# Attention and routed feed-forward on one core: rewritten for 32-row head groups, with the second half of the products for the maxima in front of the output projection

## The reference

```python
# x, ctx: (128, 128, 256), 128 batch elements of 128 tokens; 16 heads of 16 columns
q = (layernorm(x) @ Wq.T + bq) * 16 ** -0.5
k, v = ctx @ Wk.T + bk, ctx @ Wv.T + bv            # heads split
x = x + (softmax(q @ k.T) @ v) @ Wo.T + bo
# routed FFN on the 16,384 tokens, 32 experts, hidden 64
n = layernorm(x)
e = argmax(n @ router_w.T + router_b)
x = x + relu(relu(n @ w1[e] + b1[e]) @ w2[e] + b2[e])
```

## Time and profile before

| | |
|---|---|
| median of 3 runs | 2137.03 us (2135.17 to 2138.63) |
| span of the profiled execution | 2137.2 us, 51280 instructions |
| PE busy | 1898.6 us (89%) x18624 |
| PEld busy | 1418.2 us (66%) x18624 |
| DVE busy | 1553.0 us (73%) x4242 |
| ACT busy | 1209.9 us (57%) x2241 |
| POOL busy | 604.0 us (28%) x532 |
| granted clock of PE in 40 slices | tenths: 8, 7, then 9 up to slice 31, 6, and 5 in the last eight |

### The profile page before, as it was taken

The page is one execution under the profiler, slowest core; times in us unless marked ns, Lnnn a source line. Parts: engine busy times, 40 slices in busy tenths (PEclk is TensorE's granted clock), DMA queues, the critical chain, the costliest instruction groups (busy, mean ns, idle before and its releaser), DMA issues.

```text
span 2137.2 us, 51280 instructions
## 1 busy us (share of the span) xinstructions
PE 1898.6 (89%) x18624; PEld 1418.2 (66%) x18624; DVE 1553.0 (73%) x4242; ACT 1209.9 (57%) x2241; POOL 604.0 (28%) x532
## 2 busy tenths in 40 slices
PE   3699998989898989898989989898999399999998
PEld 2577776767676767676767767676777266666665
DVE  4488888878888888788878888888887444444443
ACT  2476666667666667666766666666667022222222
POOL 4112222222232222222222222222310134444444
PEclk8799999999999999999999999999999655555555
DMA  7800000111111110001000000011000333333320
GB/s 267 280 21 32 32 31 32 36 35 33 32 41 32 41 32 31 32 31 32 31 32 32 32 32 31 32 39 35 31 11 12 85 100 100 100 100 99 98 72 22
DMA packets 64060, 119.28 MB, mean 56 GB/s; under 512 B 8433, under 2 KB 45692, under 8 KB 63614
## 3 DMA queue, kind: packets, MB, share of 16 engines
q1 hardware_dynamic: 44734, 60.65, 9.5%
q0 software_dynamic: 19072, 55.15, 7.4%
HBM read 60.65 MB, written 59.31 MB: 56 GB/s over the span
## 4 chain that ended last, share of the span: by engine, by line
PE 63%; DVE 21%; issue 11%; POOL 3%; DMA 1%; DVEq 0%; SPq 0%; POOLq 0%; another core or an unknown queue 0%; ACT 0%
PE sc L812 13%; PE sc L988 9%; PE b L980 8%; PE b L826 6%; DVE mx L492 5%; DVE work L558 5%; PE sc L810 5%; PE b L773 4%; PE b L833 4%; PE b L973 3%; PE sc L791 3%; PE b L847 3%; PE b L782 2%; DVE rz L534 2%; DVE st L549 1%
## 5 line engine op out<-in xcount | busy, mean ns | idle before, releaser
L385 ACT ACTIVATE qM<-qT,cst 128x512 fp32r<-128x512 f32 x1024 | 640.0, 710 | 0.0
L812 PE MATMUL sc<-qM,kT 128*128 128x512 f32 x1536 | 518.8, 432 | 0.0
L310 POOL DMA_INDIRECT pages<-row,slot_i x128 | 129.0, 1008 | 1183.5 <-DVE slot_i L635 1151.1
L395 ACT ACTIVATE pv<-sc 128x512 f32<-128x512 f32 x512 | 295.6, 594 | 127.1 <-PE sc L812 122.0
L492 DVE TENSOR_REDUCE mx<-sc 128x4 bf16<-128x512 f32 x512 | 318.0, 684 | 53.1 <-issue 39.3
L812 PEld LDWEIGHTS sc<-qM,kT 128*128 128x128 f32 x1536 | 254.5, 193 | 16.5
L343 POOL DMA_INDIRECT out<-work x160 | 193.2, 1207 | 237.0 <-DVE work L725 234.2
L810 PEld LDWEIGHTS sc<-mxT,sel_b 128*128 128x128 bf16 x2048 | 116.7, 98 | 172.9 <-issue 124.1
L810 PE MATMUL sc<-mxT,sel_b 128*128 128x128 bf16 x2048 | 204.9, 223 | 25.1 <-DVE mxT L529 25.0
L534 DVE RECIPROCAL rz<-b 128x256 f32<-128x256 f32 x128 | 223.7, 1748 | 0.7 <-PE b L826 0.7
L988 PE MATMUL sc<-xs,rz 65*128 65x256 f32 x320 | 195.2, 714 | 0.0
(11 more groups left out here) (119 smaller groups left out, 3158.7 us busy)
## 6 DMA issues: line engine op xcount, KB each, us to landing
pages<-empty POOLq DMA_DIRECT2D x8, 2600.0 KB, 23.2
work<-pages SPq DMA_DIRECT2D x40, 520.0 KB, 3.9
xs<-x_in SPq DMA_DIRECT2D x32, 512.0 KB, 3.5
work<-ctxT SPq DMA_DIRECT2D x32, 512.0 KB, 3.3
out<-work POOLq DMA_INDIRECT x160
pv<-w SPq DMA_DIRECT2D x1, 2080.0 KB
w1s<-w SPq DMA_DIRECT2D x1, 2064.0 KB
pages<-row,slot_i POOLq DMA_INDIRECT x128
```

What stands on the lines that cost most here:

```text
L385: ins = act.activation(qM[:, u % 2, :, :, h, :], qT[:, par, :, :, u * P:(u + 1) * P].bitcast(F32), ACT.Copy, scale=cst[:, C_MASK + h:C_MAS ...
L395: act.activation(pt[:, u % 2, j], sc[j][:, :], ACT.Exp).then_inc(S["exp_out"], 1)
L812: ins = pe.matmul(sc[j][:, :], kT[:, par, a, c, u * P:(u + 1) * P], qM[:, u % 2, b, c, 4 * (j % 2):4 * (j % 2) + 4, :].rearrange("p h t -> ...
```

## The change

**Attention.** Heads are taken by row groups of 32 rows (`32 * g`), two heads to a group with two masks: `qM` is no longer eight masked copies but two, made straight from the projection with a scale and a bias, and `kT` and `qM` are plain fp32 without low parts. `scores` is eight fp32 matmuls (16 instructions) of 32 rows, 128 columns, 256 wide; `subtract_max` sixteen bf16 ones of 32 rows; `scores_for_max` two halves of eight bf16 ones of 32 rows into two banks (`mb`), the first half early in the unit, **the second directly in front of `project_out`**. `attend` is sixteen matmuls; the ones stand in `vs` beside the values, so that sums come out in the same product, and DVE normalises (`normalise`): a 32x32 block transpose of 128x512, a reciprocal of 128x16, a product, a transpose back of 128x256. The copy of the values and both norms' rows move to ACT, the router's places mostly to POOL, the residual comes two units late. The stage's loop has four steps to a turn instead of two, and the empty pages are written in pieces by SP (40 ahead, then 4 a step) and no longer all by POOL at the start.

**Pages.** The second weights stay in SBUF and TensorE reads the expert's number into a register; the first weights of a page come from HBM by a DMA of SP (`load_w1`, a ring of eight), which reads the number too. Both are padded, so that every matmul of a page has 128 rows and 128 columns. DVE copies no weights any more.

```diff
+            def load_w1(n, r, first):
+                if not first:
+                    apart(sp, ("h_out", n - (W1R - 1)))
+                e = sp.value_load(table[0:1, bass.ds(n, 1)], min_val=0, max_val=E - 1)
+                sp.dma_start(w1p[:, r % W1R, 0:2 * HID + 1],
+                             w1[:, bass.ds(e, 1), :].rearrange("p e h -> p (e h)")).then_inc(S[f"w1_in{r % W1R}"], 16)
+
...
-            def masks(q, par, u, at):
...
-                for h in range(8):
-                    ins = act.activation(qM[:, u % 2, :, :, h, :], qT[:, par, :, :, u * P:(u + 1) * P].bitcast(F32), ACT.Copy,
-                                         scale=cst[:, C_MASK + h:C_MASK + h + 1])
-                ins.then_inc(S["mask_out"], 1)
...
+                    for m in range(2):
+                        ins = act.activation(qM[:, par, m, c], pA[:, :], ACT.Identity,
+                                             scale=cst[:, C_MASK + m:C_MASK + m + 1], bias=bqm[:, m, c:c + 1])
+                ins.then_inc(S["proj_out"], 1)
...
+            def normalise(q, u):
                 after(dve, "PV_done", 4, q, u)
-                dve.reciprocal(rz[:, :], b7[:, 2 * P:4 * P]).then_inc(S["inv_out"], 1)
+                dve.transpose(tr[:, :], pB[:, :]).then_inc(S["tr_out"], 1)
+                after(dve, "tr_out", 4, q, u)
+                dve.reciprocal(inv[:, :], tr[:, :].rearrange("p (k r) -> p k r", r=32)[:, :, HD]).then_inc(S["inv_out"], 1)
                 after(dve, "inv_out", 4, q, u)
...
-                dve.tensor_tensor(aT[:, u % 2].rearrange("p c t -> p (c t)"), b7[:, 0:2 * P], rz[:, :], ALU.mult).then_inc(S["aT_out"], 1)
...
+                        maxima(s, u, 1)
...
+                        residual(q2, k2, u2, at2)
...
+                        mxT_copy(s, u)
...
+                        normalise(q1, u1)
+                    if has(atn, 0):
+                        maxima(qn, un, 0)
...
+            def scores_for_max(par, u, half_):
+                for j in range(4):
+                    for i in range(2):
+                        g, m, c = 2 * half_ + i, j // 2, j % 2
+                        rows = slice(32 * g, 32 * g + 32)
+                        ins = pe.matmul(mb[i][:, j * P:(j + 1) * P], qMh[rows, par, m, c, u * P:(u + 1) * P],
+                                        kTh[rows, par, c, u * P:(u + 1) * P], start=True, stop=True)
                 ins.then_inc(S["S_done"], 1)
...
+            def scores(par, u):
+                for c in range(2):
+                    for g in range(4):
+                        rows = slice(32 * g, 32 * g + 32)
+                        dst = sc[g][:, :].rearrange("p (m c t) -> p c m t", m=2, c=2)[:, c]
+                        pe.matmul(dst, kT[rows, par, c, u * P:(u + 1) * P], qM[rows, par, :, c, u * P:(u + 1) * P],
+                                  start=(c == 0), stop=False, skip_group_check=True)
+
+            def subtract_max(q, u):
+                after(pe, "mxT_out", 4, q, u)
+                for pair in ((0, 1), (2, 3)):
+                    for j in range(4):
+                        for g in pair:
+                            rows = slice(32 * g, 32 * g + 32)
+                            ins = pe.matmul(sc[g][:, j * P:(j + 1) * P], sel_b[rows, j, :], mxT[rows, :],
+                                            start=False, stop=True, skip_group_check=True)
+                            if j == 3:
+                                ins.then_inc(S["T_done"], 1)
+
+            def attend(par, b, u):
                 for j in range(4):
...
-                        if (a, b) == HI_LO[-1]:
-                            if j == 0:
-                                after(pe, "mxT_out", 4, q, u)
-                            for h in range(4):
-                                pe.matmul(sc[j][:, h * P:(h + 1) * P], sel_b[:, 4 * j + h, :], mxT[:, u % 2, :],
-                                          start=False, stop=False, skip_group_check=True)
-                        ins = pe.matmul(sc[j][:, :], kT[:, par, a, c, u * P:(u + 1) * P],
-                                        qM[:, u % 2, b, c, 4 * (j % 2):4 * (j % 2) + 4, :].rearrange("p h t -> p (h t)"),
-                                        start=((a, b) == HI_LO[0]), stop=((a, b) == HI_LO[-1]))
-                    ins.then_inc(S["T_done"], 1)
...
-            def attend(q, par, u):
-
-                for part in range(2):
-                    for c in range(2):
-                        for m in range(2):
-                            for j in range(4):
-                                h = 8 * c + 2 * j + m
-                                w = (vs[:, par, u, 4 * c + j].rearrange("p a d -> p (a d)")[:, 32 * m:32 * m + 32] if part == 0
-                                     else cst[:, C_ONES + 32 * m:C_ONES + 32 * m + 32])
-                                ins = pe.matmul(b7[32 * j:32 * j + 32, (2 * part + c) * P:(2 * part + c + 1) * P], w,
-                                                pt[:, u % 2, h // 4, h % 4 * P:(h % 4 + 1) * P], start=(m == 0), stop=(m == 1))
+                    for g in range(4):
+                        h = 8 * (j % 2) + 2 * g + j // 2
+                        ins = pe.matmul(pB[32 * g:32 * g + 32, j * P:(j + 1) * P], vs[:, par, u, h, :], pt[:, b, g, j, :],
+                                        start=True, stop=True)
                 ins.then_inc(S["PV_done"], 1)
 
...
+                        scores(k % 2, u)
...
+                        attend(k1 % 2, u1 % 2, u1)
                     if has(at, 0):
+                        subtract_max(s, u)
+                    if has(atn, 0):
+                        if un == 0:
+                            after(pe, "proj_out", 4, qn, 3)
+                        scores_for_max(kn % 2, un, 0)
...
+                        project(pq, (k + (2 if u == 3 else 1)) % 2, n)
+                    if has(at, 1):
+                        if has(at, 0):
+                            after(pe, "exp_out", 16, s, 4 * u)
+                        elif u:
+                            after(pe, "V_out", 4, s + 1, u - 1)
+                        values(s + 1, (k + 1) % 2, u)
...
+                    if has(atn, 0):
+                        after(pe, "max_out", 8, qn, 2 * un)
+                        scores_for_max(kn % 2, un, 1)
                     if has(at1, 0):
-                        after(pe, "exp_out", 16, q1, 4 * u1 + 3)
...
             def page_first(n, r):
+                pe.wait_ge(S[f"w1_in{r % W1R}"], (n - r % W1R) * (16 // W1R) + 16)
                 after(pe, "pT_out", 1, n, 0)
-                bank = b6 if r % 2 == 0 else b7
                 for i in range(2):
-                    ins = pe.matmul(bank[0:HID, 0:P], w1p[:, r % PN, i * HID:(i + 1) * HID], pnT[:, r % 2, i * P:(i + 1) * P],
+                    ins = pe.matmul(sc[2 + r % 2][:, 0:P], w1p[:, r % W1R, i * HID:i * HID + P], pnT[:, r % 2, i * P:(i + 1) * P],
                                     start=(i == 0), stop=(i == 1))
...
             def page_second(n, r, first):
-                after(pe, "h_out", 1, n, 0)
+                e = pe.value_load(table[0:1, bass.ds(n, 1)], min_val=0, max_val=E - 1)
                 if not first:
                     after(pe, "po_out", 1, n - 4, 0)
-                pe.matmul(sc[r % 4][:, 0:D], hT[:, r % 2, :], w2p[:, r % PN, :], start=True, stop=True).then_inc(S["y_done"], 1)
-
-            after(pe, "rk_out", 1, NQ - 1, 0)
+                after(pe, "h_out", 1, n, 0)
+                pe.matmul(mid[r % 4][:, 0:D], hT[:, r % 2, :], w2s[:, bass.ds(e, 1), :].rearrange("p e d -> p (e d)"),
+                          start=True, stop=True).then_inc(S["y_done"], 1)
```

More of the change, by code:

```diff
@@ L269, in _ @@
-            pool.wait_ge(S["pool_init"], 7)
+            pool.memset(half[:, :], -0.5).then_inc(S["pool_init"], 1)
+            pool.memset(mx[:, :], 0.0).then_inc(S["pool_init"], 1)
+            for a in range(2):
+                ins = pool.memset(vs[:, a, :, :, HD:2 * HD], 1.0)
+            ins.then_inc(S["pool_init"], 1)
+            pool.memset(empty[:, :], 0.0).then_inc(S["pool_init"], 1)
+            pool.memset(room[:, :], 0.0)
+            pool.memset(nxt[:, :], 0.0).then_inc(S["pool_init"], 1)
@@ new lines, in rank_copy, with scan @@
+            def rank_copy(q):
+                after(dve, "rk_done", 1, q, 0)
+                ranks = sc[1][:, 0:QB * E].rearrange("p (u e) -> p u e", u=QB)
+                dve.tensor_tensor(fits[:, :, :], ranks, each(room), ALU.is_ge)
+                dve.tensor_tensor(slots_old[:, :, :], ranks, each(nxt), ALU.add)
+                dve.tensor_copy(total[:, :], sc[1][:, QB * E:(QB + 1) * E]).then_inc(S["fits_out"], 1)
+            def scan(q, par, at):
+                after(dve, "fresh_out", 1, q, 0)
+                dve.tensor_tensor_scan(run[:, par, :], fresh[:, :], zer[:, :], run[:, 1 - par, E - 1:E],
+                                       ALU.add, ALU.add).then_inc(S["scan_out"], 1)
```

1091 lines of the change are left out of this document (518 added, 573 removed).

## The result

The changed kernel takes 1349.37 us (median of four runs, 1348.4 to 1350.59) where the kernel before takes 2137.83 in the same comparison: a ratio of 0.6315, with a 95% interval of 0.6306 to 0.6324. The forecast was 1435 us in a range of 1300 to 1600. The time lies inside the range and in the direction forecast, but outside the likeliest case's own range (1370 to 1510), between that case and rival A (1307).

A forecast was written before the change was run, and what follows sets the result against it. Before the change TensorE was taken to set both stages. Forecast: start 44 + attention 128 x 8.5 (1088, TensorE still the bound) + between 40 + pages 256 + end 7 = 1435 us, range 1300 to 1600.

The forecast's parts named there:

- likeliest case: Whole kernel: attention units of 8.5 us bound by TensorE, pages of 1.6; 1435 us, own range 1370 to 1510, chance 0.56.
- rival A: Attention scores: row groups overlap wholly, 0.86 us; TensorE 7.3, DVE and hand-overs bound at 7.5 a unit; 1307 us, chance 0.12.
- the scores: Attention unit on TensorE: sixteen instructions take 1.8 us, as their weight loads go in one after another.
- The changes of form: Attention unit on TensorE: the array's form changes about eight times, at 0.09 us each, 0.7 a unit.
- Is TensorE still the bound: Attention unit: DVE's sum of 7.1 us and the loop through both engines, 7.2, stay below TensorE's 8.5.
- I cost the placement at nothing: Attention: second half for the maxima before the out projection costs nothing, as the 7.2 us loop is below 8.5.
- The pages: Pages stage: full products bring the clock to about 1.00; a page takes 1.6 us (bounds 1.5 and 2.62), 256 for 160.
- rival B: Pages stage: the clock stays at 0.50; 2.2 us a page, 1531 us, chance 0.14.
- Rival C: Attention unit: scores one after another (3.4 us) or DVE's transposes twice as dear; 10.1 a unit, 1640 us, chance 0.15.
- Rival D: Attention stage: the clock falls to 0.50 through narrower forms; 16.1 us a unit, 2408 us, slower than before, chance 0.03.

The follow-up runs named there:

- Run 2: Changed kernel with the scores' matmuls issued row group by row group instead of around the four groups: 1522.81 us, no control in its group.
- Runs 3 and 4: Changed kernel with one more DVE operation a unit, before the first half's reductions (1560.06 us) or behind them in the gap (1517.73 us); no control in the group.
- run 11: Changed kernel with the out projection before the second half for the maxima and page loads issued three pages earlier: 1336.12 us, control 1349.57.
- run 6: Changed kernel with the pages' products narrow as before, 64 columns in the first and 65 rows in the second: 1647.76 us, control 1539.4.
- run 12: Changed kernel with one scatter a step instead of four, leaving out the routing of three quarters of the tokens: 1343.75 us, control 1349.57.
- run 10: Changed kernel with POOL's four scatters of a step issued apart, among POOL's other work: 1370.23 us, control 1349.57.

## Why the prediction was right, and where it was wrong

- **Right in direction, and in part in mechanism.** The work on TensorE fell and a page runs at the full clock, as forecast. By stages: start 44 forecast, 44.3 measured; between 40 and 43; pages with the end 263 and 253; attention 1088 and 1008. Of the miss of 86 us, 80 lie in attention. There the likeliest case was not what happened: rival A was, with its overlap of the row groups, its TensorE at 7.3 and its hand-overs of DVE as the bound at 7.5, and I gave it 0.12. The time stands inside the stated range because that range reached down to this rival, not because the likeliest case held.
- **The term that was mis-sized is the scores**, 1.8 us by loads one after another; measured 1.07. It is 0.7 a unit, 93 us in 128. Rival A named the reason. Run 2 shows that not even the order of groups matters.
- **The changes of form** (0.7) don't appear as a term of their own. From one start to the next, as in the earlier trace rows, some pieces are dearer than forecast: out projection 1.06 for 0.86, attend 1.02 for 0.90, the products for the maxima 0.65 for 0.5. Project is 1.50 for 1.47 and values 0.71 to 0.80 for 0.80; the subtraction is cheaper, 0.23 for 0.5. What is dearer may be changes of form, together 0.5; no run tells. The pieces of a unit sum to 6.9 us, and to 7.2 with `logits` and `ranks` (1.3 in each step of four units), against my 8.4 with changes of form. The 0.3 forecast for these two was right by luck, since 1.88 us once in four units, from which I took it, is 0.47.
- **"Is TensorE still the bound" failed in part.** I had the loop at 7.2, under TensorE's 8.5, but built it of the wrong members: through both reductions, the residual and the work of the gap. The loop that closes is the shown one, with out projection, scores and transposes in it, 7.44. With TensorE at 7.2 instead of 8.5, the two are nearly level. Runs 3 and 4 show it: 0.38 us of DVE work costs 0.33 to 0.46 in the loop, and 0.26 or nothing in the gap.
- **"I cost the placement at nothing" was wrong by a little.** The wait before the second half is there, 0.39 to 0.48 in two of four units. With the out projection in front about 10 us go, of the 13.5 of run 11. The 788 us owe nothing to the placement.
- **The pages: the forecast's case was right, rival B was not**, and run 6 shows the reason to be the one given. A page of 1.53 is near 1.6, but the price was right by luck: the 1.5 came from POOL's row writes (1.51), and what bounds is SP's sequence, for which I had a read of 0.42 and no sum. It happens to be 1.51 too. POOL's row writes now average 0.99, where I took 1.21.
- **Rival C** fell: DVE's transposes took 0.70 and 0.45 (0.62 and 0.31 assumed), and `normalise` 1.9 with its hand-overs. **Rival D** fell: 0.98 in attention, though much of the work is in forms of 32 rows or columns.

What stays open: why the same kernel has two times, 1349 and 1539. The groups ran on different chips and at different times, and no run parts the two. Shown is where the time goes, in the unit with POOL's scatters and in the pages, where POOL writes too. That these writes are the cause is a guess from the place: the run that was to test it came where there was nothing to see. Instructions that come late, the other theory of run 12, stand untested beside it.

## What to carry to other kernels

Sum one engine's pieces, but close every loop between engines over the program's real order, too: the pieces behind a hand-over (here out projection, scores and transposes) belong to it. When operands fit in 32 rows, count the time of one row group's own instructions, 0.86 of 1.07 here, and not loads one after another. Look at what POOL does beside each DVE operation on the chain before you move its work (run 10). Pad narrow products where TensorE stays at half clock though it is busy, and take a control in every group of runs before you believe that an edit costs 100 us.

## What the runs showed of the hardware that I had not expected

- Products padded from 64 columns and 65 rows to 128 do more work in less time: 2.64 a page at a granted 0.50, against 1.93 at 0.94 on the same chip.
- In the unit with POOL's four scatters PE, DVE and ACT stand still, and the unit takes 4 us more, in one group of runs and not at all in another, with the same kernel; that the scatters do it is not shown. The kernel before shows a milder form in its own trace: in the unit in which POOL issues the four scatters, one of four, both halves of `attend` together mostly take 3.7 us, in the others 1.89. Its median is within 0.3% the same in every group, so the ratio of the two kernels is 0.63 or 0.72.
- A DVE product of 128x256 that reads two tiles, 0.42 us alone, lasts until 0.3 us after the end of a POOL addition of 128x1024 during which it begins: 0.80 to 1.19 us, 25 times out of 25 in run 10.
- The turn of the loop's body adds 1.5 to 2.8 us to each of two units, every sixteen units, in the changed kernel; in the kernel before, whose turn is eight units, mostly 1.3 to 1.9. Part of it is a granted clock of 0.50 after TensorE stood still for 2.26 us.
